# Conv, attention and experts on one core: key and query tokens in two runs side by side, and half of the strip transfers issued by ScalarE

## Reference

```python
x = x + conv(group_norm(x))         # one channel per group
t = tokens(x)                       # 3136 tokens of 32 channels per image
t = t + attention(layer_norm(t))    # softmax(q k / sqrt(32)) v + its input
t = t + experts(layer_norm(t))      # top 2 of 8
out = from_tokens(t)
```

```python
xp = jnp.pad(x, ((0, 0), (0, 0), (0, 0), (6, 6)))
t1 = jnp.stack([xp[..., 2 * k:2 * k + w] for k in range(7)], axis=2)
t2 = _conv(x, w2, (0, 1))
t3 = jnp.einsum('nakhw,nbhw->nakb', t1, x) / math.sqrt(h * w)
t2p = jnp.pad(t2, ((0, 0), (0, 0), (3, 3), (0, 0)))
t4 = jnp.stack([t2p[:, :, k:k + h, :] for k in range(7)], axis=2)
t7 = _conv(t2, w7, (0, 2), groups=c)
t8 = _conv(x, w8, (4, 4), dilation=(2, 2), groups=c)
t10 = jnp.einsum('nakb,nakhw->nbhw', p9w * p6w * t3, t4) / math.sqrt(c * 7)
return t8 - (t10 - t7)
```

## Time and profile before

| | us |
|---|---|
| three timed runs | 2888.14, 2888.21, 2882.81 |
| their median | 2888.14 |
| the profiled execution | 2885.98 |
| its span, first to last instruction | 2884.2 |
| of it, `prepare` (to the last store of queries) | 630.5 |
| mean granted PE clock | 0.898 |

### The profile page before, as it was taken

One profiled execution on the slowest core, in us unless ns is written; L12 is line 12 of the kernel. 1 busy time (PEld: TensorE's weight loads), 2 busy tenths in 40 slices (PEclk: granted clock), 3 DMA queues, 4 the chain that ended last, 5 costly groups with the idle time before them and its releaser, 6 DMA issues. The chain is left out here.

```text
span 2884.2 us, 48428 instructions
## 1 busy us (share of the span) xinstructions
PE 2469.7 (86%) x18630; PEld 992.9 (34%) x18630; DVE 2398.6 (83%) x4268; ACT 1661.1 (58%) x2202; POOL 353.0 (12%) x442
## 2 busy tenths in 40 slices
PE   3877777636999999999999999999999987877776
PEld 2332323211222222222222222222222227666665
DVE  4575758458999999999999999999999946888787
ACT  1243434343777777777777777777777772333322
POOL 0010101110000000000000000000000002554545
PEclk9988889856999999999999999999999995676666
DMA  7775757251011013011011011011010001322220
GB/s 180 181 234 182 225 175 209 79 190 42 1 57 51 7 58 117 1 57 57 1 57 57 1 57 57 1 57 57 14 45 24 24 23 57 102 68 75 93 67 23
DMA packets 58941, 221.00 MB, mean 77 GB/s; under 512 B 15911, under 2 KB 28835, under 8 KB 52067
## 3 DMA queue, kind: packets, MB, share of 16 engines
q1 hardware_dynamic: 54242, 197.61, 22.2%
q0 software_dynamic: 3280, 16.80, 1.6%
q10 hardware_dynamic: 1200, 3.69, 0.4%
HBM read 81.67 MB, written 74.60 MB: 54 GB/s over the span
## 5 line engine op out<-in xcount | busy, mean ns | idle before, releaser
L1229 DVE TENSOR_REDUCE at_XM<-at_psX 128x1 f32<-128x448 f32 x2688 | 1546.3, 620 | 90.0 <-PE at_psX L1092 69.3
L1158 ACT ACTIVATE at_PR<-at_psS 128x896 f32<-128x896 f32 x1344 | 1162.9, 915 | 449.2 <-PE at_psS L1072 447.2
L1110 PE MATMUL at_psV<-at_PR,at_V 128*32 128x448 f32 x5376 | 645.2, 552 | 0.1
L1072 PE MATMUL at_psS<-at_US,at_KS 128*128 128x448 f16 x2688 | 636.1, 356 | 0.6 <-ACT at_PR L1158 0.2
L1092 PE MATMUL at_psX<-at_KS,at_US 64*128 64x448 f16 x1344 | 490.4, 365 | 61.8 <-DVE at_XM L1229 43.0
L1092 PE MATMUL at_psX<-at_KS,at_UH 64*128 64x448 f16 x1344 | 490.4, 365 | 0.0
L1092 PEld LDWEIGHTS at_psX<-at_KS,at_US 64*128 64x128 f16 x1344 | 124.5, 93 | 718.0 <-DVE at_XM L1229 661.9
L1072 PEld LDWEIGHTS at_psS<-at_US,at_KS 128*128 128x128 f16 x2688 | 200.8, 98 | 273.2 <-ACT at_PR L1158 118.6
L1496 POOL TENSOR_TENSOR fi_WE<-fi_WE 128x256 f32<-128x256 f32 (+1 forms) x224 | 212.9, 978 | 172.4 <-DVE fi_WE L1550 171.5
L1207 POOL CAST at_mrow<-at_mt 7x128 f16<-7x128 f32 x64 | 17.9, 279 | 1654.8 <-DVE at_mt L1248 1654.8
L374 PE MATMUL psA<-sb_stacks,sb_lhs 128*32 128x448 f32 x1568 | 178.9, 577 | 25.0 <-DVE sb_X L786 25.0
(11 more groups left out here) (193 smaller groups left out, 2163.5 us busy)
## 6 DMA issues: line engine op xcount, KB each, us to landing
sums<-at_O SPq DMA_DIRECT2D x16, 1568.0 KB, 6.3
fi_SUMS<-sums SPq DMA_DIRECT2D x16, 1568.0 KB, 6.6
sb_stacks<-sb_T SPq DMA_DIRECT2D x64, 270.5 KB, 7.3
sb_stacks<-sb_Xp SPq DMA_DIRECT2D x64, 248.8 KB, 8.5
sb_stacks<-sb_Xp SPq DMA_DIRECT2D x64, 248.0 KB, 5.7
at_KS<-key_stacks SPq DMA_DIRECT2D x16, 784.0 KB, 7.8
at_US<-query_stacks SPq DMA_DIRECT2D x16, 784.0 KB, 10.5
sb_stacks<-sb_T SPq DMA_DIRECT2D x64, 172.5 KB, 6.3
```

The lines of the kernel that those rows point to most:

```text
L1072: last = nc.tensor.matmul(psS[:, at % 2, k, 0:TILE], KS[:, b, (2 * c + k) * P:(2 * c + k + 1) * P], US[:, b, t * TILE:(t + 1) * TILE], sta ...
L1110: last = nc.tensor.matmul(psV[C * q:C * q + C, 0:TILE], V[:, b, G * k + q, :], PR[:, (n * 2 * STEPS + 2 * q4 + q // 2) % PRS, q % 2, :], s ...
L1158: nc.scalar.activation(PR[:, f % PRS], psS[:, at % 2, :, 0:TILE], ACT.Exp).then_inc(p_ready, 1)
L1229: nc.vector.tensor_reduce(o, psX[:, (at + j) % 3, 0:TILE], AX.X, ALU.max).then_inc(x_done, 1)
```

## The change

**Tokens in two runs.** The 25 chunks become 13 pairs: chunk j of the first run (tokens 0 to 1663) and chunk j of the second share one 128-column block, as high and low of the one and high and low of the other. So `turn_keys` makes 13 transposes in two sets, `keys` copies 1024 and 640 columns, `high_parts` is one copy of 832 columns, the copy in `low_parts` goes. `mstack` becomes two matrices, `mhi` and `mlo`, with zeroed blocks (ten more small memsets in the setup, four fewer); a query tile has 416 columns, is one of four, and takes two matmuls. DRAM holds 128x1664 of keys and of queries per image instead of 128x3136. TK holds two images, so only images 2 and 3 go through DRAM.

**Issues.** `fill_stacks2` moves from SP's list to ACT's: the upper 16 between `squares` of image 0 and the first `turned`, the lower 16 after the last `to_t2` and before the second half's `turned`.

**Order.** Images 1 and 2 are centred, scaled and split earlier in DVE's list, the T2 taps are cut up, and the keys and queries of images 1 to 3 take other places in PE's list.

**`attend`.** A load is 19 DMAs: each of the two runs brings its keys twice (64 rows each) and three pieces of the queries, each as 32 rows and once more as 31 rows (without its first row). The rows this leaves out are zeroed by memsets on POOL (DVE for image 0), for which PE waits. The loads of values stay.

```diff
-ORDER_0, ORDER = 15, 55
+ORDER_0, ORDER = 15, 51
...
-        "ks": scratch("key_stacks", (N, P, T), F16),
-        "us": scratch("query_stacks", (N, P, T), F16),
+        "ks": scratch("key_stacks", (N, P, TQ), F16),
+        "us": scratch("query_stacks", (N, P, TQ), F16),
...
-        mstack = sb("mstack", [P, P], F16)
+        mhi, mlo = sb("mhi", [P, P], F16), sb("mlo", [P, P], F16)
...
+        TK, XH = sb("TK", [P, 2, NC, C]), sb("XH", [P, 2 * JC * C])
+        Y16, US, KS = sb("Y16", [P, TQ], F16), sb("US", [P, TQ], F16), sb("KS", [P, TQ], F16)
...
-            def fill_stacks2(g, h):
-                a, z = (0, YS_CUT) if h == 0 else (YS_CUT, YS_LEN)
-                sp.wait_ge(t2_ready, g * NT + (3 if h == 0 else NT))
-                for n, s in STRIP_ORDER:
-                    sp.dma_start(T2S[C * s:C * s + C, n, a:z],
-                                 T2[C * n:C * n + C, YW * s + a:YW * s + z]).then_inc(t2s_in[h], 16)
...
-                    sp.wait_ge(tok_out, m * 16 + 16)
-                    fill_stacks2(g, 0)
...
-                    fill_stacks2(0, 0)
-                fill_stacks2(g, 1)
-                if old:
-                    store_stacks(m, 1)
+                if old:
+                    store_stacks(m, 1, first[1])
+                    store_keys(m, 2, first[2])
...
-                for q in range(min(8, NC - 8 * s)):
-                    last = nc.tensor.transpose(o[:, q * P:(q + 1) * P], z.Y16[:, 8 * s + q].rearrange("p s c -> p (s c)"),
-                                               ident16[:])
+                for q in range(min(8, JC - 8 * s)):
+                    j = 8 * s + q
+                    last = nc.tensor.transpose(o[:, q * P:(q + 1) * P], z.Y16[:, j * P:(j + 1) * P], ident16[:])
                 last.then_inc(k_full, 1)
...
-                nc.tensor.matmul(psQ[:, (KSETS + i) % 3, 0:TILE], mstack[:], z.KS[:, i * TILE:(i + 1) * TILE],
-                                 start=True, stop=True).then_inc(q_full, 1)
+                    pe.wait_ge(ks_ready, (r + 1) * KSETS)
+                elif i == 3:
+                    pe.wait_ge(u_ready, r * QSETS + 1)
+                o, k = psQ[:, (KSETS + i) % 3, 0:QTILE], z.KS[:, i * QTILE:(i + 1) * QTILE]
+                nc.tensor.matmul(o, mhi[:], k, start=True, stop=False)
+                nc.tensor.matmul(o, mlo[:], k, start=False, stop=True).then_inc(q_full, 1)
...
-                between = {2: keys_of(2), 3: queries_of(2), 5: keys_of(3), 6: queries_of(3)}
+                between = {2: keys_of(2), 3: queries_of(2), 4: keys_of(3), 5: queries_of(3)}
...
+            def fill_stacks2(g, h):
+                a, z = (0, YS_CUT) if h == 0 else (YS_CUT, YS_LEN)
+                act.wait_ge(t2_ready, g * NT + (3 if h == 0 else NT))
+                for n, s in STRIP_ORDER:
+                    act.dma_start(T2S[C * s:C * s + C, n, a:z],
+                                 T2[C * n:C * n + C, YW * s + a:YW * s + z]).then_inc(t2s_in[h], 16)
...
-                for s in (0, 2):
-                    nc.scalar.activation(z.Y16[:, :, s, :], z.XH, ACT.Copy).then_inc(y_high, 1)
-
-            def keys(m, n, z=first):
+            def high_parts(m, n, z):
+                r = m * G + n
+                if r >= 1:
+                    act.wait_ge(k_full, r * KSETS)
+                act.wait_ge(xh_ready, r + 1)
+                nc.scalar.activation(z.Y[:, :, :, 0, :], z.XR, ACT.Copy).then_inc(y_high, 1)
...
+                for i in range(3):
+                    to_t2(g, i)
+                if old:
+                    squares(m, 0, first[0])
+                if old:
+                    act.wait_ge(conv5_full, g * NT)
+                fill_stacks2(g, 0)
+                turned(g, 0, 0)
+                if old:
+                    deviations(m, 0)
+                turned(g, 1, 0)
+                if old:
+                    high_parts(m, 0, first[0])
+                turned(g, 2, 0)
+                if old:
+                    keys(m, 0, first[0])
+                turned(g, 3, 0)
+                for i in range(3, NT):
+                    to_t2(g, i)
+                    if old:
+                        query_high(m, 0, (i - 3,), first[0])
+                if old:
+                    act.wait_ge(tok_out, m * 16 + 16)
+                fill_stacks2(g, 1)
+                turned(g, 0, 1, slice(0, 2))
+                if old:
+                    squares(m, 1, first[1])
+                turned(g, 0, 1, slice(2, None))
+                turned(g, 1, 1, slice(0, 2))
+                if old:
+                    deviations(m, 1)
+                turned(g, 1, 1, slice(2, None))
+                if old:
+                    high_parts(m, 1, first[1])
+                    keys(m, 1, first[1])
+                turned(g, 2, 1)
+                if old:
+                    query_high(m, 1, (0, 1), first[1])
+                turned(g, 3, 1)
+                if old:
+                    query_high(m, 1, (2, 3), first[1])
+                    for n in (2, 3):
...
-            link(nc.vector.tensor_copy(mstack[:], mfull[:]))
-            link(nc.vector.tensor_tensor(mstack[P // 2:P], mfull[P // 2:P], mstack[P // 2:P], ALU.subtract))
-
-            for s in (1, 3):
-                link(nc.vector.memset(mstack[C * s:C * s + 1, :], 0.0))
-                link(nc.vector.memset(mstack[:, C * s:C * s + 1], 0.0))
+            link(nc.vector.tensor_copy(mhi[:], mfull[:]))
+            link(nc.vector.tensor_tensor(mlo[:], mfull[:], mhi[:], ALU.subtract))
+
+
+            for w in (mhi, mlo):
+                for h in range(2):
+                    for q in range(2):
+                        a = (2 * q + 1 - h) * C
+                        link(nc.vector.memset(w[P // 2 * h:P // 2 * h + P // 2, a:a + C], 0.0))
+                    link(nc.vector.memset(w[P // 2 * h + C:P // 2 * h + C + 1, :], 0.0))
+            link(nc.vector.memset(XH[:, NC * C:], 0.0))
...
-                link(nc.vector.tensor_tensor(z.Y16[:, :, 1, :], z.XH, z.Y16[:, :, 0, :], ALU.subtract))
-                link(nc.vector.tensor_copy(z.Y16[:, :, 3, :], z.Y16[:, :, 1, :]))
-                dve.wait_ge(y_high, r * 2 + 2)
-                nc.vector.memset(z.Y16[:, :, :, 0:1], 1.0).then_inc(y16_ready, 1)
+                dve.wait_ge(y_high, r + 1)
+                link(nc.vector.tensor_tensor(z.Y[:, :, :, 1, :], z.XR, z.Y[:, :, :, 0, :], ALU.subtract))
+                nc.vector.memset(z.Y16.rearrange("p (a c) -> p a c", c=C)[:, :, 0:1], 1.0).then_inc(y16_ready, 1)
...
-                taps_row((0, 1))
+                taps_row((0,))
+                if old:
+                    scale(m, 1, z)
+                    taps_row((1,))
+                    low_parts(m, 1, z)
+                    taps_row((2,))
+                    query_low(m, 1, z)
                 mixing(g)
                 if old:
-                    query_low(m, 1, tiles=range(0, 3))
+                    z = first[2]
+                    centre(m, 2, z)
                 new_weights(g)
                 if old:
-                    query_low(m, 1, tiles=range(3, NT))
-                taps_row((2, 3, 4))
+                    scale(m, 2, z)
+                else:
+                    taps_row((1, 2))
+                add((0,))
+                if old:
+                    low_parts(m, 2, z)
+                add((1,))
+                taps_row((3, 4))
                 dve.wait_ge(taps_done, g + 1)
-                add((0,))
-                if old:
-                    centre(m, 2)
-                add((1,))
-                if old:
-                    scale(m, 2)
-                    low_parts(m, 2)
                 add((2,))
+                if old:
+                    query_low(m, 2, z)
+                    z = first[3]
+                    centre(m, 3, z)
+                add((3,))
+                if old:
+                    scale(m, 3, z)
+                if old:
+                    low_parts(m, 3, z)
...
-        LOADS = 6
+        LOADS = 19
...
-                for dst, src in ((KS[:, b], scr["ks"][n]), (US[:, b], scr["us"][n]),
-                                 (UH[HALF:P, b], scr["us"][n, 0:HALF]),
+                ks, us = scr["ks"][n], scr["us"][n]
+                parts = []
+                for r, (a, z) in enumerate(((0, TQ), (TQ, T))):
+                    k = ks[HALF * r:HALF * r + HALF, 0:z - a]
+                    hi, lo = (us[HALF * h + C * r:HALF * h + C * r + C, 0:z - a] for h in range(2))
+
+                    parts += [(KS[0:HALF, b, a:z], k), (KS[HALF:P, b, a:z], k), (US[0:C, b, a:z], hi),
+                              (US[C + 1:HALF, b, a:z], hi[1:C]), (US[HALF:HALF + C, b, a:z], lo),
+                              (US[HALF + C + 1:P, b, a:z], lo[1:C]), (UH[HALF:HALF + C, b, a:z], hi),
+                              (UH[HALF + C + 1:P, b, a:z], hi[1:C])]
+                for dst, src in (*parts,
...
+                    if m == 0:
+                        pe.wait_ge(zeroed, 3)
+                    else:
```

(53 more changed lines are left out.)

244 lines of the change are left out of this document (110 added, 134 removed).

## The result

The changed kernel takes 3033.52 us (median of four runs, 3030.96 to 3034.88) beside 2887.26 us before: 1.051 times as long, 95% interval 1.0491 to 1.0527, or 146 us slower. The profiled execution has a span of 3033.1 us. Forecast was 2950 (2900 to 3015): the sign was right, the size was not, and the time lies 18.5 us above the range.

A forecast was written before the change was run, and what follows sets the result against it. Bound by hand-overs between engines in `prepare`, where none is full, and by when loads land in `attend`. 2885.98 + 30.3 (`prepare`) + 33 (`attend`'s start) + 0 (steady loads) = 2949.3, taken as 2950 us; range 2900 to 3015.

The forecast's parts named there:

- The step that failed: Steady loads in `attend`: slack before the maxima's rows under 1 us, cost taken as 0; otherwise up to 5 us per image.
- a rival at 58 us: Maxima's rows wait behind each steady load in `attend`: 13 x 4.5 = 58 us, total 3000 to 3015; chance 0.18.
- The start of `attend`: Maxima's transfer queues behind three loads of 27.9 us each on one DMA engine; scores start 33 us later (27 to 40).
- ACT's issues: T2 strips on ACT in `prepare`: 0.75 us each, 12.0 upper and 13.5 lower batch, 25.5 us on a group's first half.
- the two rivals with cheap or free issues: Strips on ACT: issues cost 0.42 us each, 2903, chance 0.10; or issues don't hold ACT, 2850, chance 0.05.
- The sentence weighed against it: Counter-argument on the price of ACT's issues: by that rule the move would be about nothing, total near 2850.
- Inside a group: Groups in `prepare`: `mixing` at t 85.9, image 3 split t 120.2, next first tap t 146.4; next strips 4.1 us late.
- 7.0, 12.3 and 6 together: Three groups of `prepare`: longer groups +7.0 us, late next strips +12.3 (0 to 20), PE's lower clock +6 (0 to 15).
- Group 0: First group of `prepare`: no stall goes in return for ACT's issues, +17.5 us; the setup's extra memsets are a separate +1.4.
- The drain: End of `prepare`: 3.0 us less for each of three images, plus savings on the first, tail and last store: -13.9 us.
- The 31-row rule: Loads in `attend`: one DMA engine carries 31-row pieces at 25 GB/s, 583 KB in 23.3 us, 27.9 us per load.
- The rival that spreads the pieces: Loads in `attend`: pieces spread over all engines, load 5 us longer, not 33, total 2922; chance 0.05.

The follow-up runs named there:

- experiment 1: Changed kernel with each 31-row piece of `attend`'s loads cut into 16 and 15 rows (25 DMAs per load, same bytes): 2929.55 us.
- experiment 4: Kernel before with only the two query transfers of a load cut into pieces of 33 and 31 rows (10 DMAs per load): 2950.63 us.
- experiment 5: Changed kernel with only the second run's three 31-row pieces cut into 16 and 15 rows, the first run's kept: 2937.36 us.
- experiment 6: Changed kernel with the transfers of the maxima's rows issued by POOL instead of SP, loads still in 31-row pieces: 2967.86 us.
- experiment 2: Changed kernel with both batches of T2 strips issued by SP again, at their former places: 2940.38 us.
- experiment 7: Changed kernel, only upper strips on ACT: 2981.87 us; changed kernel with pieces cut to 16 and 15 rows, only lower strips on ACT: 2888.94 us.
- experiment 8: Kernel before with one edit, both batches of T2 strips issued by ACT; tokens, loads and orders stay: 2997.85 us.

## Why the prediction was off

**The step that failed** is the one on the steady loads: "The slack is under 1 us: I take **0**". The mechanism behind it was described right, and stood as a rival at 58 us, but it was set aside on a difference between two numbers that I did not know to 1 us. The difference also left out the rows' own landing: with the 2 us that the rival counts for it, 853.2 becomes 855.2, behind the 854.03 at which they are wanted. The single engine's load was priced at 27.9 us and 3.9 for the sums, 31.8; in the trace it is busy from 902.6 to about 938, some 35.5, the next rows included. The rows waited, and that gives 66.5 us: 13 waits of 3.3 and 1.8 each at the lower clock behind them, which no step had. With the rival as forecast case the sum would have been 3008, inside the range; some 26 us more come from terms that were sized too small: 9.5 in `prepare`, 8.9 at the start of `attend` and 8.5 in the steady part. Experiments 1, 4 and 5 confirm the mechanism, and experiment 6 that the rows wait in SP's queue.

**The start of `attend`**: +33 forecast, +41.9 measured. It was taken as three loads of 27.9 us; the first lands 34.3 us behind its issue and the rows get through 93.2 us behind it, 31 a load. That is the same mis-sized term, 3 us a load too small. The picture of a row that is issued in time and queues behind the third load was incomplete: SP could not issue it before 757.17, as its own issues had slowed to 1.45 us each, a cost that no step had.

**ACT's issues**: 0.75 us each taken, measured 0.69 for the upper and 0.95 for the larger lower ones (11.03 and 15.26 for 16), where I had 12.0 and 13.5. The choice of 0.75 over ACT's own single issue of 0.42 was right, and the two rivals with cheap or free issues are refuted by experiments 2, 7 and 8. The 0.29 us a strip from which the last one would have made the kernel faster was never near. The sentence weighed against it, that issuing elsewhere saves only the sequencer's time, small beside the transfer (Trainium skill, "DMA: Bandwidth & Descriptors", section "Issuing engines are not separate DMA queues"), misleads here: one issue of 0.7 to 0.95 us is small beside the 6 to 12.6 us until it lands, but 32 of them on the chain cost 23 us a group.

**Inside a group** the steps hold. In group 2 the next strips are late: the first copy to T2 starts at 320.18, t 8.9, 4.6 us later in the group than before (4.1 forecast). The forecast kept these 4.1 us out of its times t; with them added (in brackets) it compares so: `mixing` at t 92.1 (90.0), image 3 split at t 127.5 (124.3), the stall 8.23 (7.9), the next first tap at t 153.75 (150.5). Over groups 1 to 3 the loss is 29.7 us against 25.3 (7.0, 12.3 and 6 together). Group 0 costs 19.1 beside the setup's 1.4 (17.5 and 1.4). The drain gives 10.3 back, not 13.9. These three are off the same way, by 4.4, 1.6 and 3.6 us, 9.5 in sum.

**The 31-row rule**: one engine carries such a piece (Trainium skill, same page, section "Why a DMA increments its semaphore by 16 and not by 1"); the trace agrees with some 25 GB/s left over and experiment 1 with 104 us gained by 16 and 15 rows. (The prediction's "one for a prime" is short for what the Trainium skill states there, the largest divisor up to 16; for 31 that is one.) The rival that spreads the pieces is refuted.

Left open is how the 35.5 us of that engine divide: 583 KB at 25 to 26 GB/s are 22.4 to 23.3, so by an estimate its share of the wide transfers takes 12 to 13 us instead of the 8.4 that I had for it, but no run measured it alone.

## What to carry to other kernels

A transfer's rows decide how many DMA engines work on it; a piece of 31 rows is better issued as 16 and 15. Where something small and urgent shares a queue with a long transfer, ask when the slowest engine is through, and where the slack is smaller than the error of that figure, take the loss into the forecast or price the range by it. A batch of 16 issues of T2 strips cost SP and ACT about the same (0.64 to 0.99 us each), so put it on the engine that nobody waits for. And the price of an issue is no constant: on SP's list the issues of a load took 0.52 us each with the pieces cut and 1.45 with the 31-row pieces, so a slow DMA engine also holds back the list that feeds it.

## What the runs showed of the hardware

The steady loss was larger than PE's waits: 3.3 us of standing still cost another 1.8 at the lower clock, with matmuls at 0.55 instead of 0.36 us; waits of 1.7 us (experiment 4) cost only another 0.4. Rows issued on POOL's queue landed 5.5 us later while three loads of SP's queue were under way. SP's issues slowed from 0.52 to 1.45 us each while one DMA engine was behind. And the rate of that one engine, 25 to 26 GB/s, was the same with rows of 6272 bytes and of about 3000.
